# A decoder's latent attention: two divisions go from GpSimd to VectorE, and the end of each pair of sequences is put in another order

## The reference

```python
q_latent = hidden_states @ Wqa                        # 192 latents of each query
q = (q_latent @ Wqb).reshape(b, s, 16, 128)           # 64 plain + 64 rotated channels
kv_comp = hidden_states @ Wkva
c_kv, k_pe = kv_comp[..., :64], kv_comp[..., 64:]     # 64 latents of keys and values + 64 rotated
q_pe, k_pe = _apply_rope(q_pe, cos, sin), _apply_rope(k_pe, cos, sin)
scores = einsum('bhqd,bhkd->bhqk', q_full, k_full) * 128 ** -0.5   # causal
probs = softmax(scores)
out = einsum('bhqk,bhkd->bhqd', probs, v)  @ Wo
```

## Time and profile before

| | |
|---|---|
| median of 3 runs | 723.18 us (721.86 to 723.79) |
| the profiled execution | 724.21 us, span 722.4 us |
| PE busy | 558.2 us, 77% of the span |
| DVE busy | 430.5 us, 60% |
| ACT busy | 300.2 us, 42% |
| POOL busy | 253.3 us, 35% |
| TensorE clock granted, mean | 0.883 of full |

### The profile page before, as it was taken

How to read it: one execution, slowest core, us unless ns; L and a number is a source line. 1 busy time by engine, 2 the same in 40 slices (tenths; PEclk the granted TensorE clock), 3 DMA queues, 4 the chain that set the end, 5 groups by cost and what they waited for, 6 DMA issues and landing times.

```text
span 722.4 us, 12069 instructions
## 1 busy us (share of the span) xinstructions
PE 558.2 (77%) x4141; PEld 394.7 (55%) x4143; DVE 430.5 (60%) x994; ACT 300.2 (42%) x742; POOL 253.3 (35%) x297
## 2 busy tenths in 40 slices
PE   3949699258369999999979989979888367763665
PEld 2538344156248888887635656656575155643233
DVE  3586899946545555554572544535465647767773
ACT  1421200242534444443423745727573455545553
POOL 3950478854700000000576954908622200010000
PEclk9969999655679999999988999999999789885886
DMA  8592410444751111110220000000000500000000
GB/s 293 171 371 95 145 59 0 150 157 149 243 189 53 46 46 45 46 44 24 81 88 1 1 0 1 1 0 1 1 1 1 175 2 2 2 2 0 8 22 30
DMA packets 32248, 49.62 MB, mean 69 GB/s; under 512 B 3096, under 2 KB 22368, under 8 KB 31808
## 3 DMA queue, kind: packets, MB, share of 16 engines
q1 hardware_dynamic: 29888, 41.65, 17.4%
q0 software_dynamic: 2304, 7.21, 2.8%
HBM read 39.68 MB, written 9.18 MB: 68 GB/s over the span
## 4 chain that ended last, share of the span: by engine, by line
PE 58%; DVE 18%; ACT 12%; POOL 4%; issue 4%; DMA 3%; SPq 0%; ACTq 0%; DVEq 0%; POOLq 0%
PE bank L1565 14%; PE bank L1580 4%; PE bank L1735 4%; PE bank L1675 3%; POOL sorted_rows L499 3%; PE bank L1697 3%; PE bank L1671 2%; PE bank L1724 2%; PE bank L1443 2%; PE bank L1708 2%; ACT sm L722 2%; ACT pT L824 2%; DVE xn L930 2%; PE bank L1980 2%; PE bank L1472 1%
## 5 line engine op out<-in xcount | busy, mean ns | idle before, releaser
L667 ACT ACTIVATE hf<-bank,be 128x256 f32<-128x256 f32 (+1 forms) x120 | 44.3, 420 | 67.4 <-PE bank L1565 53.4
L505 POOL DMA_INDIRECT yg<-expert_rows,pos x16 | 15.8, 988 | 156.0 <-DMA expert_rows<-yb 151.5
L1565 PE MATMUL bank<-h,wsp 128*128 128x256 f16 (+1 forms) x720 | 67.6, 249 | 1.7 <-DVE h L1123 1.6
L1565 PEld LDWEIGHTS bank<-h,wsp 128*128 x720 | 57.2, 97 | 11.1 <-issue 4.8
L1121 DVE CAST h<-hf 128x512 f16<-128x512 f32 (+1 forms) x60 | 21.8, 364 | 56.6 <-ACT hf L667 55.2
L487 POOL TENSOR_TENSOR kvp<-xnT,cxT 128x512 f32<-128x512 f32 x32 | 35.7, 1139 | 42.8 <-issue 33.3
L577 ACT CAST wsp<-wraw 128x2048 f16<-128x2048 f32 x12 | 22.7, 1900 | 66.6 <-DMA wraw<-in_L_ffn_W 66.6
L722 ACT ACTIVATE sm<-sm,nm 128x128 f32<-128x128 f32 x128 | 49.9, 395 | 0.6 <-DVE nm L1236 0.6
L465 POOL TENSOR_TENSOR wsp<-wraw,wsp 128x512 f16<-128x512 f32 x40 | 45.8, 1178 | 9.1 <-ACT wsp L577 8.8
L1233 DVE SCALAR_TENSOR_TENSOR sm<-bank,const 128x512 f32<-128x512 f32 x32 | 22.1, 691 | 38.9 <-PE bank L1697 38.9
L524 POOL TENSOR_TENSOR sm<-sm,rinv 128x512 f32<-128x512 f32 x32 | 33.1, 1040 | 24.9 <-DVE rinv L1227 24.9
(11 more groups left out here) (299 smaller groups left out, 1337.3 us busy)
## 6 DMA issues: line engine op xcount, KB each, us to landing
wraw<-in_L_ffn_W SPq DMA_DIRECT2D x16, 512.0 KB, 5.2
wraw<-in_L_ffn_W SPq DMA_DIRECT2D x8, 1024.0 KB, 7.0
cxT<-in_ctxT SPq DMA_DIRECT2D x2, 1024.0 KB, 7.6
tap<-in_taps SPq DMA_DIRECT2D x1, 2048.0 KB, 14.1
xg<-sorted_rows SPq DMA_DIRECT2D x8, 256.0 KB, 2.8
expert_rows<-yb SPq DMA_DIRECT2D x8, 256.0 KB, 2.2
sorted_rows<-early POOLq DMA_DIRECT2D x1, 1536.0 KB, 13.1
sorted_rows<-early POOLq DMA_DIRECT2D x1, 1408.0 KB, 16.3
```

Source lines behind the costliest of these rows:

```text
L667: last = nc.scalar.activation(hf[:, p, n * k:n * k + n], bank[2 * (layer - 1) + p][:, n * k:n * k + n], ACT.Gelu, bias=be[:, layer - 1, u, ...
L1565: last = nc.tensor.matmul(b[:, n * (f % 2):n * (f % 2) + n], w[a_][:, c, P * f:P * f + P], inp[:, b_, c, :], start=(c == 0 and a_ + b_ == ...
```

## The change

Four things are changed in `pair4`, and nothing outside it:

- the divisions of groups 6 and 7 are no longer on POOL's queue but on DVE's, each behind the inversion of its sums; they have a semaphore of their own, p4_divided, for which PE's turn_p(i, 1, 2) and turn_p(i, 1, 3) now wait;
- on DVE, copy_pT(i, 5) no longer stands behind the inversion of group 7, rope_k(after, 0) stands ahead of the last copy, copy_pT(i, 7), and add_tile(i, 0) ahead of quantise_weights(i);
- on PE, key_latents(after, 0) stands ahead of output(i, 0), and turn_p(i, 1, 2) and turn_kv(after, 0) between its halves; likewise key_latents(after, 1) ahead of output(i, 1), and turn_kv(after, 1) between its halves;
- turn_q(after, 0, 0), the first turn of the next pair's queries, is issued behind values(i, 1) and not at the next pair's start.

```diff
 POOL, pair4:
-                divide(i, 6)
-                divide(i, 7)
 DVE, pair4:
                 invert(i, 6)
+                divide(i, 6)
+                copy_pT(i, 5)
                 invert(i, 7)
-                for j in range(5, 8):
-                    copy_pT(i, j)
+                divide(i, 7)
+                copy_pT(i, 6)
+                if after is not None:
+                    rope_k(after, 0)
+                copy_pT(i, 7)
                 if after is None:
                     for t in range(NT - 2):
                         stats(5, t)
+                add_tile(i, 0)
                 quantise_weights(i)
-                for u in range(2):
-                    if after is not None:
-                        rope_k(after, u)
-                    add_tile(i, u)
+                if after is not None:
+                    rope_k(after, 1)
+                add_tile(i, 1)
 PE, turn_p:
-                pe.wait_ge(sem("p4_ready"), i * 8 + (4 * u + g + 1))
+                j = 4 * u + g
+                if j < 6:
+                    pe.wait_ge(sem("p4_ready"), i * 6 + (j + 1))
+                else:
+                    pe.wait_ge(sem("p4_divided"), i * 2 + (j - 5))
 PE, pair4:
-                turn_q(i, 0, 0)
+                if i == 0:
+                    turn_q(i, 0, 0)
                 turn_keys(i)
...
                 values(i, 0, after)
                 turn_p(i, 1, 1)
-                output(i, 0, 0, 4)
-                output(i, 0, 4, 8)
-                turn_p(i, 1, 2)
                 if after is not None:
                     pe.wait_ge(sem("oT_ready"), i * 4 + 2)
                     key_latents(after, 0)
-                turn_p(i, 1, 3)
+                output(i, 0, 0, 4)
+                turn_p(i, 1, 2)
                 if after is not None:
                     turn_kv(after, 0)
+                output(i, 0, 4, 8)
+                turn_p(i, 1, 3)
                 values(i, 1, after)
+                if after is not None:
+                    turn_q(after, 0, 0)
+                    pe.wait_ge(sem("oT_ready"), i * 4 + 4)
+                    key_latents(after, 1)
                 output(i, 1, 0, 4)
                 if after is not None:
-                    pe.wait_ge(sem("oT_ready"), i * 4 + 4)
-                    key_latents(after, 1)
-                output(i, 1, 4, 6)
-                if after is not None:
                     turn_kv(after, 1)
-                output(i, 1, 6, 8)
+                output(i, 1, 4, 8)
```

More of the change, by code:

```diff
@@ L1227, in invert, with divide @@
                 nc.vector.reciprocal(rinv[:, u, 4 * g:4 * g + 4], rsum[:, u, 4 * g:4 * g + 4]).then_inc(sem("r4_ready"), 1)
+            def divide(i, j):
+                u, g = steps[j]
+                hs = slice(4 * g, 4 * g + 4)
+                dve.wait_ge(sem("r4_ready"), i * 8 + (j + 1))
+                nc.vector.tensor_tensor(sm[:, u, hs, :], sm[:, u, hs, :],
+                                        rinv[:, u, hs].unsqueeze(2).to_broadcast([P, 4, P]), ALU.mult).then_inc(sem("p4_divided"), 1)
             def pair4(i, after):
```

## The result

| | before | changed |
|---|---|---|
| median of 13 runs each (lowest to highest) | 723.7 us (721.31 to 727.65) | 712.62 us (710.78 to 721.23) |
| the profiled execution | 724.21 us, span 722.4 | 710.82 us, span 709.0 |
| latent attention, from its first turn of queries to the first transpose behind it | 390.13 to 558.98: 168.9 us | 385.00 to 547.23: 162.2 us |

The ratio of the changed kernel to the one before is 0.986 (95% interval 0.983 to 0.989), faster by 1.4% or some 10 us. Two executions of the kernel before in the later comparisons took some 981 us at a granted clock of 0.553; every ratio here leaves them out.

A forecast was written before the change was run, and what follows sets the result against it. PE's 9.4 us idle before the second values, mostly waiting for DVE's rope_k, was taken as the bound. 724.21 - 5.2 - 1.65 = 717.4, or 716.3 to 718.0 from the median; 717.0 was taken, range 714.6 to 719.6.

The forecast's parts named there:

- Up to the second values: PE in each pair with a successor: values starts 6.85 us after T, the start of turn_p(i, 1, 1); before 8.72, 9.24, 7.65.
- The new wait for oT: PE's key_latents(after, 0) waits 0.4 us until ACT has copied both halves of the first oT from banks 7 and 0.
- DVE: Both divisions priced at nothing: DVE is 0.8 us early for the last copy; beside POOL a division takes 0.74 to 1.56.
- The sum of the waits: Shorter waits before the second values: gains of 1.87, 2.39, 0.80 and 0.15 us in pairs 0 to 3, together 5.2.
- Behind values: From second values to the next latents: 7.55 us against 7.53, priced at nothing, bounds 0.3 gain or loss per pair.
- The clock: Pair 1's values after the standstill should keep full clock instead of 1.2 GHz: up to 1.65 us more.
- The range's allowance: 1.5 us to either side, for low-clock stretches behind latent attention falling otherwise when those stages start 7 us earlier.
- More than forecast: Rival: a stretch of low clock behind latent attention vanishes as well, giving 713 to 715 us; chance 10%.

The follow-up runs named there:

- the later comparisons: The kernel before and the changed kernel run again without edits, twice beside each other; changed against before gave ratios 0.988 and 0.989.
- With the clock held up the kernel before: The kernel before with 20, 24 and 12 unread transposes in PE's waits before the second values of pairs 0 to 2; ratios 0.998 and 0.9956 to before.
- the second trace: Profile of the kernel before, run again with no edit: ratio 0.9993 to before, latent attention 385.1 to 557.2 us.
- a variant: Three of 1.8, one of 1.91: changed kernel plus four DVE reductions before copy_pT(i, 6), 0.988 to before. Six of 1.3: kernel before, quantise_weights moved, 0.989 twice.

## Why the prediction was wrong in its size

- *Up to the second values*: T + 6.91, forecast T + 6.85. The new wait for oT is there (0.23 us idle by the trace; 0.44 from T + 0.44, where PE could have gone on, forecast 0.4), and so are all the starts between. From one pair's turn_p(i, 1, 1) to the next it is 43.3 us, forecast 43.2.
- *DVE*: the division of group 6 beside POOL's rotation took 1.06 us (forecast up to 1.56), that of group 7 0.76, each between the bounds. DVE waits 0.87 us ahead of the last copy, forecast 0.8. The rule of the Trainium skill that spoke against the move ("SBUF — State Buffer", Who interferes with whom), that such a division contends with a GpSimd instruction that reads SBUF, agrees with the trace: the quickest of the eight divisions, in pair 3 with POOL idle, took 0.69 us, and POOL's two rotations beside the slow one 1.44 us instead of 0.99. As forecast, it changed nothing in the sum.
- *The sum of the waits*: 5.2 us forecast. With the clock held up the kernel before takes 167.2 us in latent attention and the changed one 162.2: 5.0.
- *Behind values*: 7.57 us, forecast 7.55. Only the total holds; of its two parts one costs 0.7 us and one gives it back, as the kernel without the move of turn_q shows.
- *The clock*: this is the step that failed, as a mis-sized term. From the one stretch at 1.2 GHz of the one trace I took between 0 and 1.65 us for the clock and counted 1.0. The two traces of the kernel before show one and three stretches, and kept at work its PE gains 1.7 and 3.2 us, 2.4 in the mean. The three stretches of the second trace are 5.0 us. Standstills of 2.97 and 1.91 us, which I had taken for harmless, were followed by them too.
- *What this term does not explain*: 5.0 and 2.4 make 7.4 us. Had I counted so, the forecast would have been some 716 us, still above the 712.62 measured, and so the clock in latent attention accounts for 1.4 to 2.2 us of the 4.4 by which I was off. The first comparison gave 9.9 us (7.7 to 12.1), the two later ones 8.8 and 8.3. On the chip where all were run together, 5.1 and 3.2 make up the 8.3 measured. Where the rest comes from, 2 to 3 us of the first result, stays open; no trace places it in latent attention, which took 162.2 us in all three traces of the changed kernel.

The range's allowance of 1.5 us to either side was made for stretches in later stages. That stretches of the stage itself could be more than one, which points only one way, had no term. My case *More than forecast* (10%) had the direction, but gave a stretch behind the stage as its cause, which the traces neither show nor exclude.

## What to carry to other kernels

Before a queue is rearranged, look for work without a near reader that stands ahead of work with one: moving the weights' quantisation behind the key's rotation, one line, gave all but 0.5 of the 6.6 us by which the whole rearrangement shortened the stage. A standstill of TensorE of 1.9 to 3.5 us cost its own length and, in four of the six of the kernel before, a stretch at half clock after it; one trace tells the price of such a stretch but not how often it comes, so take its count from several executions or reach with the range to one behind each standstill. A sum of two moves that comes to nothing is not two moves that are worth nothing.

## What the runs showed of the hardware

- In latent attention the low clock was granted only to a PE at work again: in the second execution of the kernel before the clock stood at 1.00 through all three standstills, and at 0.62, 0.75 and 0.53 in the 3.0, 2.5 and 3.6 us behind them. That is no rule: ahead of latent attention, in a standstill of 4.32 us of the first trace, the clock was at 0.51 over the last half microsecond before PE went on.
- It came after standstills of 1.91, 2.97 and 3.50 us and stayed away after 1.90 and 2.97 in another execution of the same program, in a variant after three of 1.8 and one of 1.91, and after six of 1.3. So the length of a standstill alone does not tell.
- Transposes of a constant, 0.11 us each, kept it away in all six waits of two executions, with 0.6 to 0.9 us of each wait left idle.
- The same code brought the kernels to latent attention between 384.9 and 390.1 us, in fourteen traces.
